# Causal mask added by one product per bank instead of four, and the second bias split on eight partitions

## The reference

```python
h = combined @ W                      # embedding by position, nesting and segment
q = layernorm(h) @ wq + bq; k = ...; v = ...
logits = (q / 8) @ k.T                # per head, 128 x 128
logits = where(k_pos <= q_pos, logits, -1e10)     # one block of 128: plain causal
h = h + softmax(logits) @ v @ wo + bo
logits_r = layernorm(h) @ router_w.T + router_b   # 8 experts, top 2, softmax of the two
a = silu(x @ fc1_w[e, :256].T + b) * (x @ fc1_w[e, 256:].T + b)
y[e] = a @ fc2_w[e].T + fc2_b[e]      # fc2_b is the "second bias", 8 x 128
out = h + sum over the two experts of weight * y[e]
```

## Time and profile before

| | us |
|---|---|
| median of 3 runs | 1457.07 (1456.79 to 1458.69) |
| the profiled execution's own time | 1445.55 |
| its span, first to last instruction | 1443.5 |
| TensorE busy in the span | 1212.5 (84%) |
| VectorE / ScalarE / GpSimd busy | 1008.8 / 985.7 / 885.1 |
| mean granted clock of TensorE | 0.968 |

### The profile page before, as it was taken

How to read it: one execution, slowest core, us unless ns; L and a number is a source line. 1 busy time by engine, 2 the same in 40 slices (tenths; PEclk the granted TensorE clock), 3 DMA queues, 4 the chain that set the end, 5 groups by cost and what they waited for, 6 DMA issues and landing times. The chain is left out here.

```text
span 1443.5 us, 47446 instructions
## 1 busy us (share of the span) xinstructions
PE 1212.5 (84%) x13916; PEld 1043.9 (72%) x13917; DVE 1008.8 (70%) x3837; ACT 985.7 (68%) x3496; POOL 885.1 (61%) x1214
## 2 busy tenths in 40 slices
PE   6898899999999899999999975678887777887885
PEld 4576777777777778777777764577777777777774
DVE  6578888888778788888878864656555555565553
ACT  3797898889879889888988863445444444454442
POOL 6346776667666667667667665555555545555554
PEclk9999999999999999999999996799999999999998
DMA  5240111111111111111111111434444334333431
GB/s 162 90 171 17 37 53 39 39 56 35 52 41 36 48 43 49 41 39 56 35 52 41 48 57 46 126 112 111 112 114 116 113 101 112 113 115 106 116 112 48
DMA packets 73348, 108.59 MB, mean 75 GB/s; under 512 B 15037, under 2 KB 39301, under 8 KB 73157
## 3 DMA queue, kind: packets, MB, share of 16 engines
q1 hardware_dynamic: 53444, 63.19, 15.8%
q0 software_dynamic: 19840, 44.62, 8.8%
HBM read 46.18 MB, written 53.18 MB: 69 GB/s over the span
## 5 line engine op out<-in xcount | busy, mean ns | idle before, releaser
L775 ACT ACTIVATE probs<-ps,neg_max 128x128 f32<-128x128 f32 (+1 forms) x1024 | 338.1, 361 | 20.1 <-DVE neg_max L963 17.7
L648 POOL DMA_INDIRECT xs<-normed,row x256 | 261.6, 1022 | 81.6 <-issue 78.7
L1247 PE MATMUL ps<-xT_hi,w_now 128*128 128x256 f32 x576 | 178.8, 310 | 93.4 <-DVE xT_lo L1134 92.6
L775 ACT ACTIVATION_READ_ACCUMULATOR probs<-ps,neg_max 128x1 f32 x1024 | 232.6, 227 | 0.0
L716 ACT CAST xT_hi<-ps 128x256 fp32r<-128x256 f32 x144 | 54.8, 381 | 247.6 <-PE ps L1410 225.7
L1247 PEld LDWEIGHTS ps<-xT_hi,w_now 128*128 128x128 f32 x576 | 109.6, 190 | 110.2 <-DVE xT_lo L1134 106.1
L587 POOL TENSOR_TENSOR probs<-probs,inv_sums 128x384 f32<-128x384 f32 x120 | 99.3, 828 | 124.1 <-DVE inv_sums L913 118.3
L1249 PE MATMUL ps<-xT_hi,w_now 128*128 128x256 f32 x576 | 162.8, 283 | 0.0
L1248 PE MATMUL ps<-xT_lo,w_now 128*128 128x256 f32 x576 | 162.7, 282 | 0.0
L684 POOL DMA_INDIRECT xs<-probs,v x108 | 104.4, 967 | 88.8 <-DVE probs L1143 62.1
L684 POOL DMA_INDIRECT out_h<-probs,v x108 | 104.5, 967 | 87.9 <-DVE probs L1143 60.8
(11 more groups left out here) (244 smaller groups left out, 3305.6 us busy)
## 6 DMA issues: line engine op xcount, KB each, us to landing
v<-xs SPq DMA_DIRECT2D x102, 260.0 KB
kT<-xs SPq DMA_DIRECT2D x34, 260.0 KB
xs<-pad_rows SPq DMA_DIRECT2D x16, 520.0 KB, 3.0
normed<-h SPq DMA_DIRECT2D x32, 256.0 KB
xs<-normed,row POOLq DMA_INDIRECT x256
w_parts<-in_w SPq DMA_DIRECT2D x1, 2048.0 KB, 9.0
xs<-probs,v POOLq DMA_INDIRECT x108
out_h<-probs,v POOLq DMA_INDIRECT x108
```

Of the source, the lines that this page charges most:

```text
L648: pool.indirect_dma_start((xs[0], xs_parts)[k], bass.IndirectOffsetOnAxis(ap=row[par][:, k, j:j + 1].bitcast(U32), axis=0), normed2[par][: ...
L775: ins = nc.scalar.activation(probs_p[par][:, half, slots[n]], ps[:, SCORES + half, slots[n]], ACT.Exp, bias=neg_max[par][:, half, n:n + 1] ...
L1247: T.matmul(dst, w_hi_, x_hi_, start=True, stop=False)
```

## The change

It has four parts.

The mask: the eight products become two, one for each bank. The weights are a doubled identity of 64 rows by 128 columns (`ident_2`), the moving operand four triangles side by side (256 columns). For this the four blocks that need the mask must lie alike in the two halves of the bank, so the slots change places; the reductions and the reciprocals follow with other strides, over the same number of elements.

The second bias: a DMA brings it as 8 rows of 128. GpSimd splits it on eight partitions (`b2_split`); the clearing of `b2_parts`, half as large now, moves from the opening into the step. SP then waits for the split and copies the two parts by two DMAs into rows 0 and 1 of `b2_parts`. In `fc2` the bias is read twice by a broadcast instead of standing twice.

Two moves in the opening: on VectorE the first two edges of the table of parts go ahead of the wait for the tokens, and `xlo` of group 0 goes ahead of `embed_add` of group 1.

GpSimd's constants: one more copy of the triangle and one more piece of identity, one memset of `add_parts` less, and the clearing of `b2_parts` gone. SP no longer waits for GpSimd's constants ahead of the bias' DMA.

```diff
@@ -144,7 +144,7 @@
     steps = [(w, 0) for w in ("onehot", "split", "embed", "embed_add", "embed_r", "vtable", "stats", "rstd")] + [("onehot", 1)]
-    steps += [("norm", 0), ("normT", 0), ("embed", 1), ("embed_add", 1), ("embed_r", 1), ("xlo", 0), ("bias", 0)]
+    steps += [("norm", 0), ("normT", 0), ("embed", 1), ("xlo", 0), ("embed_add", 1), ("embed_r", 1), ("bias", 0)]
     behind = ((("stats", 1), ("rstd", 1)), (("norm", 1), ("normT", 1)), (("xlo", 1),), (("residual", 0),))
...
@@ -180,7 +180,7 @@
         ident = sb("ident", [128, 128])
-        causal = sb("causal", [128, 3, HQ], BF16); ident_b = sb("ident_b", [128, 128], BF16); triangle = sb("triangle", [128, HQ])
+        causal = sb("causal", [128, 2, 2, HQ], BF16); ident_2 = sb("ident_2", [128, 2, HQ], BF16); triangle = sb("triangle", [128, HQ])
         part_code = sb("part_code", [CODES, 1])
...
@@ -241,7 +241,7 @@
         probs_p = [t[:].rearrange("p n k -> p (n k)")[:, 0:2 * PACK].rearrange("p (e c) -> p e c", e=2) for t in probs]
-        slots = (slice(0, S), slice(S, 2 * S), slice(2 * S, 2 * S + HQ), slice(2 * S + HQ, PACK))
+        slots = (slice(0, S), slice(S + HQ, 2 * S + HQ), slice(S, S + HQ), slice(2 * S + HQ, PACK))
         probsT = sb("probsT", [S, HEADS, S])
...
@@ -275,9 +275,9 @@
         b1_all = sb("b1_all", [128, EXPERTS * 4])
-        b2_raw = masked[0][0:64].rearrange("p n k -> p (n k)").rearrange("p (e d) -> p e d", d=D)
-        b2_parts = sb("b2_parts", [128, EXPERTS, 2, D], F32R)
-        part_rows = (slice(0, 1), slice(32, 33))
+        b2_raw = sb("b2_raw", [EXPERTS, D])
+        b2_split = sb("b2_split", [EXPERTS, 2, D], F32R)
+        b2_parts = sb("b2_parts", [128, EXPERTS, D], F32R)
         add_parts = sb("add_parts", [128, 128], F32R)
...
@@ -342,7 +342,7 @@
         silu_in = led_sem("silu_in")
+        ...; s_b2 = sem("s_b2"); s_b2_in = sem("s_b2_in")
         s_zero = sem("s_zero"); wait_carried = sem("wait_carried"); s_trash = sem("s_trash")
...
@@ -415,6 +415,10 @@
                         pad_pair(st[1])
+                    if st[0] == "b2_parts":
+                        sp.wait_ge(s_b2, 1)
+                        for part in range(2):
+                            sp.dma_start(b2_parts[part:part + 1].bitcast(F32), b2_split[:, part].bitcast(F32)).then_inc(s_b2_in, 16)
                     if st[0] == "route_norm":
...
@@ -450,8 +454,7 @@
             sp.dma_start(w2[:], a["w2"]).then_inc(s_w2, 16)
-            sp.wait_ge(s_pool, 1)
-            sp.dma_start(b2_raw, a["b2"].broadcast_to([64, EXPERTS * D]).rearrange("p (e d) -> p e d", d=D)).then_inc(s_w2, 16)
+            sp.dma_start(b2_raw[:], a["b2"].rearrange("o (e d) -> (o e) d", d=D)).then_inc(s_w2, 16)
             sp.wait_ge(s_codes_more, 16)
...
@@ -515,9 +518,10 @@
             link(pool.memset(masked[0][:], 0.0))
-            link(pool.tensor_copy(ident_b[:], ident[:]))
-            for n in range(3):
-                link(pool.tensor_copy(causal[:, n], triangle[:]))
+            for rows in (slice(0, HQ), slice(HQ, S)):
+                link(pool.tensor_copy(ident_2[rows], ident[rows, rows].unsqueeze(1).broadcast_to([HQ, 2, HQ])))
+            for n in range(4):
+                link(pool.tensor_copy(causal[:, n // 2, n % 2], triangle[:]))
             link(pool.memset(ones[:], 1.0))
...
@@ -537,10 +541,8 @@
             link(pool.memset(pad_rows[:], 0.0))
-            link(pool.memset(b2_parts[:].bitcast(F32), 0.0))
             link(pool.memset(add_parts[:].bitcast(F32), 0.0))
-            for p in part_rows:
-                link(pool.memset(add_parts[p].bitcast(F32), 1.0))
+            link(pool.memset(add_parts[0:2].bitcast(F32), 1.0))
             link(pool.iota(normed2[1][:, :, TOKEN:TOKEN + 1].bitcast(I32), pattern=[[S, GB], [0, 1]], base=-GB * S, channel_multiplier=1))
...
@@ -592,13 +594,9 @@
                     pool.wait_ge(s_w2, 16 * 2)
-                    for p in part_rows:
-                        ins = pool.tensor_copy(b2_parts[p], b2_raw[p].unsqueeze(2).broadcast_to([1, EXPERTS, 2, D]))
-                        link(ins)
-                    p = part_rows[1]
-                    pool.tensor_tensor(b2_parts[p], b2_raw[p].unsqueeze(2).broadcast_to([1, EXPERTS, 2, D]), b2_parts[p].bitcast(F32),
-                                       ALU.subtract).then_inc(s_b2, 1)
-                    pool.wait_ge(s_b2, 1)
+                    link(pool.memset(b2_parts[:].bitcast(F32), 0.0))
+                    link(pool.tensor_copy(b2_split[:, 0], b2_raw[:]))
+                    pool.tensor_tensor(b2_split[:, 1], b2_raw[:], b2_split[:, 0].bitcast(F32), ALU.subtract).then_inc(s_b2, 1)
                 elif kind == "residual":
...
@@ -852,6 +850,22 @@
+            dve.wait_ge(s_const, 1)
+            p = small[:, 0:1]
+            acc, cmp_ = small[:, 1:2], small[:, 2:3]
+            n3 = PARTS * NEST
+            link(V.tensor_copy(part_code[:], p))
+            link(V.memset(acc, 0.0))
+
+            def place(edge, code_step, part_step):
+
+                link(V.tensor_scalar(cmp_, p, float(edge), None, ALU.is_ge))
+                link(V.scalar_tensor_tensor(part_code[:], cmp_, float(code_step), part_code[:], ALU.mult, ALU.add))
+                link(V.scalar_tensor_tensor(acc, cmp_, float(part_step), acc, ALU.mult, ALU.add))
+
+            edges = ((NEST, -NEST, 1), (2 * NEST, -NEST, 1), (n3, -NEST, -2), (n3 + SEG, -SEG, 1), (n3 + 2 * SEG, -SEG, 1))
+            for edge in edges[0:2]:
+                place(*edge)
             dve.wait_ge(s_x, 16)
...
@@ -872,17 +886,8 @@
-            dve.wait_ge(s_const, 1)
-            p = small[:, 0:1]
-            acc, cmp_ = small[:, 1:2], small[:, 2:3]
-            n3 = PARTS * NEST
-            link(V.tensor_copy(part_code[:], p))
-            link(V.memset(acc, 0.0))
-            for edge, code_step, part_step in ((NEST, -NEST, 1), (2 * NEST, -NEST, 1), (n3, -NEST, -2),
-                                               (n3 + SEG, -SEG, 1), (n3 + 2 * SEG, -SEG, 1)):
-                link(V.tensor_scalar(cmp_, p, float(edge), None, ALU.is_ge))
-                link(V.scalar_tensor_tensor(part_code[:], cmp_, float(code_step), part_code[:], ALU.mult, ALU.add))
-                link(V.scalar_tensor_tensor(acc, cmp_, float(part_step), acc, ALU.mult, ALU.add))
+            for edge in edges[2:]:
+                place(*edge)
             link(V.tensor_scalar(part_mask[:, PARTS:PARTS + 1], acc, 1.0, None, ALU.is_ge))
...
@@ -909,8 +914,9 @@
-                V.reciprocal(inv_sums[par][:, e, 0:4].rearrange("p (a r) -> p a r", a=2), sums[par][:, e, 0:2].unsqueeze(2).broadcast_to([S, 2, 2]))
-                return V.reciprocal(inv_sums[par][:, e, 4:6], sums[par][:, e, 2:4])
+                inverse = inv_sums[par][:, e].rearrange("p (a r) -> p a r", a=2)
+                V.reciprocal(inverse[:, :, 0:2], sums[par][:, e, 0:2].unsqueeze(2).broadcast_to([S, 2, 2]))
+                return V.reciprocal(inverse[:, :, 2], sums[par][:, e, 2:4])
...
@@ -959,9 +965,9 @@
                     dve.wait_ge(probs_ready, LEAD + b - 1)
-                    V.tensor_reduce(neg_max[par][:, :, 0:2], ps[:, SCORES:SCORES + 2, 0:2 * S].rearrange("p e (a k) -> p e a k", a=2), AX, ALU.max, negate=True)
-                    V.tensor_reduce(neg_max[par][:, :, 2:4], ps[:, SCORES:SCORES + 2, 2 * S:PACK].rearrange("p e (a k) -> p e a k", a=2), AX, ALU.max,
-                                    negate=True).then_inc(max_ready, 1)
+                    both = ps[:, SCORES:SCORES + 2, 0:PACK].rearrange("p e (a k) -> p e a k", a=2)
+                    V.tensor_reduce(neg_max[par][:, :, 0:2], both[:, :, :, 0:S], AX, ALU.max, negate=True)
+                    V.tensor_reduce(neg_max[par][:, :, 2:4], both[:, :, :, S:S + HQ], AX, ALU.max, negate=True).then_inc(max_ready, 1)
                 elif kind == "value":
...
@@ -1339,13 +1345,11 @@
                                                kT[gp][rows, pair, at:at + (S if high else HQ)], start=(n == 0), stop=False, skip_group_check=True)
-                    for part in (slice(0, 3), slice(3, 4)):
-                        for c in range(2):
-                            for e in range(2):
-                                rows, wide = slice(e * HD, (e + 1) * HD), part.stop - part.start
-                                blocks = ps[c * HQ:(c + 1) * HQ, SCORES + e, 0:PACK].rearrange("p (n k) -> p n k", k=HQ)
-                                dst = blocks[:, 1:6:2] if wide == 3 else blocks[:, 4:5]
-                                ins = T.matmul(dst, ident_b[rows, rows], causal[rows, 0:wide], start=False, stop=True, skip_group_check=True)
+                    for e in range(2):
+                        rows = slice(e * HD, (e + 1) * HD)
+                        masked_keys = ps[:, SCORES + e, 0:PACK].rearrange("p (a k) -> p a k", a=2)[:, :, HQ:S + HQ]
+                        ins = T.matmul(masked_keys, ident_2[rows].rearrange("p c q -> p (c q)"), causal[rows].rearrange("p a n k -> p a (n k)"), start=False, stop=True,
```

(5 more changed lines are left out.)

2 lines of the change are left out of this document (1 added, 1 removed).

## The result

| | changed | kernel before | ratio, 95% interval |
|---|---|---|---|
| first measurement | 1441.07 us | 1456.93 us | 0.989 [0.987, 0.991] |
| again, a second chip | 1260.03 | 1262.95 | 0.998 [0.996, 0.999] |
| again, a third chip | 1441.71 | 1454.67 | 0.993 [0.990, 0.995] |

The change is faster, by 15.9 us at first and by 2.9 and 13.0 on the other two chips, where 1460.5, 3.4 slower, was forecast. The same kernel before takes 1455 us in some of the measurements and 1262 in others. Each total time is compared only with the kernel before beside it; stages are compared between traces, and on the later slow chips the kernel before was not traced, so there they stand beside its trace in the first measurement. What differs between the two levels turned out to be what the forecast had missed.

A forecast was written before the change was run, and what follows sets the result against it. Prediction took TensorE's own pace to bound the attention loop between its waits for the input's transposes; +10.4 (mask) - 5.4 (second bias) - 1.6 (opening) = +3.4 us on the median 1457.07 gave 1460.5, range 1446 to 1469.

The forecast's parts named there:

- Two borders instead of one: TensorE between scores and transposes: the array's division changes twice, not once, 0.125 us more per paying sequence; chance 0.70.
- one border: Rival at the mask: array goes from quarters to row halves without a gap, mask costs nothing, 1450.1 us; chance 0.14.
- no border: Rival at the mask: gaps come from 32-bit weights, so the mask gains 7.5 us, 1442.6 us; chance 0.06.
- Five of eight pay: Attention loop: five of eight sequences pay in 15 octets, all eight in the last; 83 x 0.125 = +10.4 us.
- The failed step: Loop, input's transposes: waits for VectorE, 1.2 us on average, hide the mask of two sequences per octet.
- The condition I gave for being wrong: Waits before the input's transposes shrink by what the masks take, so fewer than five of eight sequences pay.
- The clock: Rival in the loop: longer octets make the granted clock fall in five more octets, +15 us, 1475; chance 0.06.
- The second bias: Octet 1: shorter GpSimd split removes TensorE's 6.06 us wait, less 0.7 for VectorE's norm; -5.4 us, bounds -6.2 and -4.5.
- The opening: Start of the kernel: earlier `rstd`, edges and `xlo` bring the first key product forward; -1.6 us, bounds 0 and -3.3.
- The broadcast operand: Expert stage's bias product: reading 128 floats twice costs nothing; as a rival, costing its columns again, +15.8 us, chance 0.04.
- The range: Whole kernel: 1446 to 1469 us, taking in most of the one border case, leaving out most of the clock.

The follow-up runs named there:

- quarters: Changed kernel with the mask as four products of 64x256 in quarters of the array; 1253.72 us (0.9927) on a quick chip, 1429.79 us (0.986) on a slow one.
- three borders: Changed kernel with one row half's mask as one product, the other's as two in quarters of the array; 1455.80 us, 1.001 of the kernel before.
- late_scatter: Kernel before with only a GpSimd memset of 128x768 ahead of the scatter of each octet's second sequence; 1442.75 us (0.992) and 1430.02 us (0.985).
- the old mask: Changed kernel with its mask edit taken back to eight products; 1254.93 us (0.993) on a quick chip, 1447.04 us (0.994) on a slow one.
- the pause: GpSimd memset of 128x768 ahead of the scatter of each octet's second sequence; on the changed kernel with quarters 1417.91 us (0.978) slow, 0.9976 quick.

## Why the prediction failed, by its steps

- **Two borders instead of one**: right. 0.15 and 0.21 us, as named; quarters and three borders confirm it from both sides. The price was mis-sized: 0.10 a sequence, not 0.125. Rivals *one border* and *no border* are out.
- **Five of eight pay**: right by sequence on the slow chip, for which it was made. Five sequences of an octet are longer by 0.06 to 0.10 us, 0.44 together; the two that wait for VectorE and the one behind the second wait are not. On a quick chip the octet grows by 0.51, which is also five times 0.10, but that is luck: the waits that were to hide the mask are missing there, and seven sequences pay 0.03 to 0.11 each. 13 octets take 6.6 us more, with the last about 7.5 against my 10.4 (the measured mask alone: 5.7).
- **The failed step** is the one that took the wait of the earlier trace rows as given: "the mask of the sequence whose transposes of the input wait for VectorE is hidden, twice, by a wait of 1.2 us on average". I read who ended that wait, VectorE, and didn't ask why VectorE was late. The row behind it, 28.5 us at "remote", was in the same view. On slow chips the wait comes with late increments, and in the changed kernel GpSimd's scatter stands past the point where those of the mask and the transposes arise in 8 of 13 octets. Octets still late take 51.2 us (50.8 before: the borders), the others 49.9. In the loop the waits lose 11.1 us (30.6 to 19.5) and the clock, next step, about 6, and the borders add 5.7: -11.4 measured, where my sum had 13 x 5 x 0.125 = +8.1. By which path the edits shift the scatter isn't shown; the mask alone frees 3 octets and the other parts alone 4, on different chips. The condition I gave for being wrong, that these waits "shrink by what the masks take", named the right place with too small a size.
- **The clock** as a rival: I had it fall more often. The kernel before has two falls, in octets 7 and 8 (53.9 and 53.7 us for 50.8), 6 us together. The changed kernel has none in its loop:

```profile
143.85:800.24 656.39, 625.82 (x7959) 513.57 (x7957) 549.32 (x2350) 587.49 (x2237) 460.37 (x680) 1.00 0.14 45
```

  That the falls lay in the wait that shortened is likely from the earlier trace rows, where the fall follows that wait, but not tested. Whether the timed runs of before all have it isn't known; the other slow traces have none or one.
- **The second bias**: right in kind, too small. -5.4 forecast; the sequence went from 14.48 to 6.38 us, -8.1 (13.59 to 6.38 on a quick chip). I had left 0.7 for a norm held by the new GpSimd work, where the norm took 1.35 for 1.11, and valued the rest by one wait, 6.06. The missing term is the lower clock behind that wait, 2.25 us.
- **The opening**: right in sum, -1.8 for -1.6 on the slow chip, -0.8 on the quick one. It is GpSimd's share; the two moves alone can't be told from nothing.
- **The broadcast operand**: right. The product takes as long as before (278/284/577 ns in the trace of before):

```profile
L1432 PE MATMUL ps<-b_parts,add_parts x144: 278/283/573, 901.6 to 1420.9; 128*128 x144
```

- **The range** was that of borders. Its lower end, 1446, had no case in which a wait goes that the edit doesn't touch. Without late increments the sum would have failed too, by less: -2.9 on the quick chip for +3.4, since the mask costs 3 to 5 us less than forecast and the second bias brings about 3 more.

What stays open: what makes an increment late on some chips and not on others; whether it is the chip at all, since each chip was measured once; why `late_scatter` gave 0.992 on one slow chip and 0.985 on the other with equal loops (646.9 and 646.4 us) — its expert stages there are 538.8 and 527.4, and that of before was not traced; and the 8 us between quarters and its expectation.

## What to carry to other kernels

Before a wait is taken as cover, follow it one engine further back: a row "<- VectorE" whose own row says "<- remote" is not a property of the schedule, and an edit elsewhere can shift it. Look at the granted clock behind every long wait that an edit removes: the time at the lower clock goes with it, here 2.25 us beside 6.06. On TensorE keep products that follow each other in one division of the array; four products in the scores' quarters do what two in row halves do, 0.10 us earlier. The second bias is what gains everywhere: alone, with the old mask or with the quarters it is at 0.992 to 0.993 on quick chips. On slow chips it gives 0.994 with the old mask, 0.986 with the quarters and 0.978 with the pause besides, but with the pause only 0.998 on a quick one.

## What was not expected of the hardware

The same program runs at 1262 us on three chips and near 1455 on two others (and in the first measurement). Each chip was measured once, so whether the chip or something else of the occasion decides isn't shown. The difference is not the clock: in the profiled executions the quick ones show 0.970 to 0.976, the slow ones 0.963 to 0.973. What differs in the traces is when the increments of TensorE's products reach other engines. In the third sequence on a slow chip the mask's increment comes 2.1 to 2.4 us behind the start of the product where it is late (changed kernel), and 0.3 us where it isn't. For the mask and the first transposes of an octet's third sequence this happens only where a scatter of GpSimd is issued ahead of them, with the edge between 1.000 and 1.007 us behind the scores, and a pause on GpSimd takes it away. For the embedding product and in the expert stage increments are late with the pause too, and what sets them off wasn't looked for. Of the 50 us between the loops of the two levels the pause takes some 21, with the two falls of the clock among them; of the 123 us between the expert stages none is explained by a run.

Whether the increment travels late or the product itself ends late, these traces can't say. The Trainium skill (Perfetto Trace Analysis, Tensor Engine Instruction) has it that the end of a product in a profile is an estimate and not observed; the trace agrees in so far as the ends shown lie 1.8 to 2.0 us ahead of their increments in the octet with late ones above, and 0.01 to 0.02 in the other.
